# Which of the state-space products GpSimd makes: pairs 0, 1, 3 in place of 0, 2, 4

## The reference

```
state = state * exp(dt[d] * A[d, n]) + (dt[d] * u[d]) * B[n]      # one step in time, 512 of them
y[d]  = sum over n of state * C[n]
y     = (y + D * u) * silu(z)          # z is the layer norm of x
x     = x + transpose(y)
```

## Time and profile before

| | us |
|---|---|
| timed runs, median (lowest, highest) | 506.89 (505.04, 507.24) |
| the profiled execution's own time | 503.0 |
| its span | 501.2 |
| VectorE busy | 469.0 |
| GpSimd busy | 453.0 |
| TensorE busy | 431.6 |
| ScalarE busy | 346.5 |

### The profile page before, as it was taken

One profiled execution on the slowest core, in us unless ns is written; L12 is line 12 of the kernel. 1 busy time (PEld: TensorE's weight loads), 2 busy tenths in 40 slices (PEclk: granted clock), 3 DMA queues, 4 the chain that ended last, 5 costly groups with the idle time before them and its releaser, 6 DMA issues.

```text
span 501.2 us, 4086 instructions
## 1 busy us (share of the span) xinstructions
PE 431.6 (86%) x1028; PEld 179.7 (36%) x1036; DVE 469.0 (94%) x368; ACT 346.5 (69%) x620; POOL 453.0 (90%) x237
## 2 busy tenths in 40 slices
PE   8749869998798669999898699879988989988797
PEld 4214323433343233434333243424433433343343
DVE  5899999999998999999998999999999977999895
ACT  2797746966579868897679767788788693643332
POOL 4379999989898999999998999999999959999992
PEclk9979989999799989999899989989999997989899
DMA  5799745429971000200981000000593000000002
GB/s 185 250 368 335 185 84 116 88 41 233 329 276 56 0 1 0 63 1 27 332 339 43 1 21 1 21 1 0 166 397 157 1 21 21 32 11 21 1 0 84
DMA packets 17871, 53.96 MB, mean 108 GB/s; under 512 B 2724, under 2 KB 3236, under 8 KB 16824
## 3 DMA queue, kind: packets, MB, share of 16 engines
q1 hardware_dynamic: 16696, 45.31, 25.0%
q0 software_dynamic: 1152, 8.39, 8.3%
HBM read 49.24 MB, written 4.46 MB: 107 GB/s over the span
## 4 chain that ended last, share of the span: by engine, by line
POOL 36%; PE 21%; DVE 19%; issue 17%; ACT 4%; DMA 1%; SPq 0%; POOLq 0%; DVEq 0%; ACTq 0%
POOL h L1104 24%; PE y L509 10%; POOL h L1097 9%; DVE dA L953 9%; DVE h L959 3%; DVE h L953 3%; PE work L486 2%; POOL dtu L1090 2%; PE work L409 2%; ACT dA L774 2%; DVE acc L910 1%; PE work L502 1%; PE work L429 1%; DMA w_in<-w_inT 1%; PE work L436 1%
## 5 line engine op out<-in xcount | busy, mean ns | idle before, releaser
L1104 POOL TENSOR_TENSOR h<-b_rep,dtu 128x1024 f32<-128x1024 f32 x127 | 301.8, 2441 | 12.5 <-DMA b_rep<-bc_scratch 11.2
L509 PE MATMUL y<-h,ident 128*128 128x512 f32 x508 | 248.4, 627 | 37.2 <-DVE h L959 35.0
L774 ACT ACTIVATE dA<-dt,a_neg 128x512 f32<-128x512 f32 x256 | 165.7, 679 | 85.1 <-DVE h L959 74.9
L953 DVE TENSOR_TENSOR_SCAN dA<-dA,h 128x1024 f32<-128x1024 f32 x83 | 189.7, 2285 | 4.8 <-ACT dA L774 4.8
L509 PEld LDWEIGHTS y<-h,ident 128*128 128x128 f32 x508 | 96.3, 198 | 173.9 <-issue 108.6
L1097 POOL TENSOR_TENSOR h<-h,c_rep 128x1024 f32<-128x1024 f32 x45 | 107.1, 2382 | 11.8 <-DVE h L953 11.7
L953 DVE TENSOR_TENSOR_SCAN h<-dA,h 128x1024 f32<-128x1024 f32 x45 | 102.5, 2280 | 4.5 <-ACT dA L774 4.5
L959 DVE TENSOR_TENSOR h<-dA,c_rep 128x1024 f32<-128x1024 f32 x82 | 99.8, 1217 | 1.2
L409 PE MATMUL work<-ctx_sb,w_in 128*128 128x512 f32 x60 | 35.0, 716 | 15.1 <-DVE x L995 14.3
L502 PE MATMUL work<-fsum,xnT 128*128 128x512 f32 x64 | 29.2, 598 | 0.0
L910 DVE SCALAR_TENSOR_TENSOR acc<-work,chan,acc 128x511 f32<-128x511 f32 (+2 forms) x30 | 21.7, 731 | 5.3 <-ACT acc L641 5.0
(11 more groups left out here) (132 smaller groups left out, 415.1 us busy)
## 6 DMA issues: line engine op xcount, KB each, us to landing
b_rep<-bc_scratch SPq DMA_DIRECT2D x32, 512.0 KB, 9.3
c_rep<-bc_scratch SPq DMA_DIRECT2D x32, 512.0 KB, 9.0
fsum<-factors POOLq DMA_DIRECT2D x8, 1024.0 KB, 8.2
x<-x SPq DMA_DIRECT2D x4, 1024.0 KB, 8.5
out<-x SPq DMA_DIRECT2D x16, 256.0 KB, 2.0
ctx_sb<-ctxT SPq DMA_DIRECT2D x3, 512.0 KB, 4.1
ctx_sb<-ctxT SPq DMA_DIRECT2D x2, 256.0 KB, 3.8
w_in<-w_inT SPq DMA_DIRECT2D x1, 384.0 KB, 4.4
```

The costliest lines, as they stand in the source:

```text
L509: mm = pe.matmul(y[:], ident[:], h[:, (s * PAIRS + j) % H_RING, i, :], start=False, stop=(j == sum_order(s)[-1] and i == 1))
L774: act.activation(dA[:, j % 2, i, :], dt[:, k % 2, :], ACT.Exp, scale=a_neg[:, k, 2 * j + i:2 * j + i + 1]).then_inc(exp_done, 1)
L953: dve.tensor_tensor_scan(pair if on_pool(s * PAIRS + j) else decay, decay, pair, 0.0, ALU.mult, ALU.add).then_inc(scanned, 1)
L1104: pool.tensor_tensor(h[:, (s * PAIRS + j) % H_RING], b_rep[:, j], dtu[:, k % 2, :].unsqueeze(1).to_broadcast([P, 2, L]), ALU.mult).then_in ...
```

## The change

Four constants are replaced. In steps 0 to 3 GpSimd makes the products with C of pairs 0 and 3 in place of 0 and 4. In steps 4 to 14 it makes those of 0, 1 and 3 in place of 0, 2 and 4. In step 15 nothing changes. VectorE makes all others; which tile the scan writes, what ScalarE waits for and what SyncE waits for follow from `on_pool`. The orders of the sums on TensorE are changed with it.

```diff
-EARLY_POOL_C = (0, 4)
-EARLY_SUM_ORDER = (1, 0, 2, 3, 5, 4, 6, 7)
-POOL_C = (0, 2, 4)
+EARLY_POOL_C = (0, 3)
+EARLY_SUM_ORDER = (1, 0, 2, 4, 3, 5, 6, 7)
+POOL_C = (0, 1, 3)
 LAST_POOL_C = (0, 2, 4, 5)
-SUM_ORDER = (1, 0, 3, 2, 5, 4, 6, 7)
+SUM_ORDER = (0, 2, 1, 4, 3, 5, 6, 7)
 LAST_SUM_ORDER = (1, 0, 3, 2, 4, 6, 5, 7)
```

## The result

The changed kernel is slower. In the first measurement its median was 512.98 us (510.57 to 514.53) against 505.97 for the old one: ratio 1.0151, 95% interval 1.0104 to 1.0198. In a second one, on other runs, 1.0189 (1.0164 to 1.0213). So +7.6 to +9.5 us, where +4.4 was forecast. The median of 512.98 lies in the stated range, the sign was right and so was most of the mechanism; the size of the change was too small by a third or more.

What follows compares the result with a forecast made beforehand. VectorE, busy 94% of the span, was taken as the bound. Terms 1.0 + 3.9 - 0.7 + 1.7 - 1.5 = +4.4 us on the profiled 503.0 gave 507.4, carried over to 511.3 us timed; range 507.6 to 514.2.

Steps and rivals of the forecast that it cites:

- The pins in even steps: Steps 4, 6, 8, 10: ScalarE's block fixes pair 4's scan, whose product with C now lies behind it; +3.9 us.
- The joints: Steps 1 to 3, 5, 7, 9, 11: VectorE's product straight behind its own scan; +0.14 us each, +1.0 us in all.
- Steps 12 and 13: TensorE idles before pair 4's sum, then runs slow, delaying the last layer and step 13; +1.7 us.
- Steps 10 and 11: Pair 1 summed third instead of pair 3, so x_proj starts sooner and two gaps on VectorE go; -0.7 us.
- Steps 14 and 15: Sums of pairs 4 and 3 fill TensorE's gap, so step 15's gate of step 14's y starts sooner; -1.5 us.
- what costs nothing: GpSimd's reordered products, as many as before, and SyncE's shifted loads: most of GpSimd's 11.7 us waiting goes, at no cost.
- rival C: GpSimd or the loads become late, 1 to 2 us each time; slower still, 515; chance 0.07.
- Rival A: Decays in even steps move forward with VectorE, so waits at pairs 4 and 5 go; faster, 501.7 us; chance 0.07.
- E3: ScalarE's two decay exponentials of pair 3; starting over 1.1 us earlier in steps 4, 8 and 12 would favour Rival A.
- Rival B: Pins cost as forecast, but TensorE stays fast in step 12 and gives it back; no change, 508.0; chance 0.20.
- The sum's ends: Terms' extremes: 3.2 us at TensorE's full clock; 8.0 without gains of steps 10, 11, 15 and step 13 at 2.9.
- the 1.2 us I gave it: Whole kernel: TensorE's throttled clock makes the total some 1.2 us dearer than at full clock.

Runs made afterwards that it cites:

- odd_only: Old kernel with the new pairs and sum order in steps 5, 7, 9, 11 and 13 alone; 3.6 us slower than the old kernel.
- even_only: Old kernel with the new pairs and sum order in steps 4, 6, 8, 10, 12 and 14 alone; 1 us more than the upper end of the expected +4.5 to +5.5.
- k0_pool045: Old kernel, but in steps 4, 8 and 12 GpSimd multiplies pairs 0, 4, 5 instead of 0, 2, 4; ratio 1.0007 to the old kernel.
- after_gate4: Changed kernel with ScalarE's four gates behind the decays of pair 4 instead of pair 3; ratio 1.0043 to the old kernel.
- early_only: Old kernel with the change in steps 0 to 3 alone; the expected +0.4 us lies in the measured interval.
- before_gate4: Old kernel with ScalarE's four gates behind the decays of pair 4 instead of pair 3; ratio 1.0018 to the old kernel.
- after_warm: Changed kernel with products of a zero matrix added where TensorE idled in steps 9 and 12; ratio 1.0071 to the old kernel.
- after_bias4: Changed kernel with GpSimd's second bias addition of step 13 one pair later, at pair 4 instead of 3; ratio 1.0105 to the old kernel.
- combined: Changed kernel with later gates, later bias addition and zero-matrix products in steps 5, 7, 9, 12 and 13; ratio 0.9937 to the old kernel, 502.9 us.

## Why the prediction was right, and what was mis-sized

- *The pins in even steps* (+3.9 us in steps 4, 6, 8, 10): shown by the traces. Behind S0, S4 of step 8 starts at 15.95 to 15.96 us and S4 of step 12 at 15.34 to 15.35 in the old kernel, odd_only, even_only and both profiles of the changed one, whichever pairs these steps have (all five with these heads at full clock), and S5 came 0.91 us later each in steps 6 and 8. Putting a product more ahead of the pin (k0_pool045) shortened the steps by 1.2 us. Moving the gates (after_gate4) gave back only 0.2 of the 0.91, as C2 then held up E4. Step 4 measured +0.49 and +1.18 instead of +1.26: in the first profile TensorE had run step 3 at a higher clock than in the earlier trace rows, so the pin itself came 0.8 sooner. early_only and odd_only, with the old pairs in step 4, show the same 0.79.
- *The joints* (+0.14 each): +0.13 to +0.16 in steps 1, 2, 3, 5, 7 and 9.
- *Steps 12 and 13* (+1.7): +1.77 and +1.55. The slow sum of pair 4 was there (granted clock 0.50 after 3.95 us of idling), and filling the gap took it away. The layer behind it came 2.4 us later against S0 of step 12, the upper end of the 1.2 to 2.4 given, and the wait for the raw layer shrank by 1.7 as allowed for. That the sum came out to 0.1 us is partly luck: early_only, with the old code, is 1.44 us shorter in these two steps.
- *Steps 10 and 11*: the two gaps went (-0.34 and -0.76 between scans), but the net was +1.8, not +0.3. The term that was mis-sized is S4 of step 10: I took the head of the chain, the last layer on TensorE, from the old trace, where step 10 began at full clock. The slow head costs 1.70 us. The old pairs don't cover it either: it costs them +1.7 in step 6 of odd_only and before_gate4 and in step 8 of early_only, and +1.34 in step 10 of k0_pool045, where S4 stands at the same 16.64 us behind S0 as in the changed kernel. What differs is how often it comes: step 10 had it in all six profiles with the new pairs there and no filling, and in one of six with the old pairs. With the head at full clock (after_warm) steps 10 and 11 are at +0.13, near the forecast.
- *Steps 14 and 15* (-1.5): the gain at the gate came (1.54 to 0.20 us of waiting) and was given back in the tail. Here the step "what costs nothing" failed: GpSimd, with 11.7 us of waiting for scans in the whole, stands still nowhere behind its wait for ScalarE in step 13, in either kernel, and its start there is set by ScalarE's chain behind S1 of step 13. In the changed kernel it began 9.95 us later and ended 10.5 us later, so what VectorE regains at the gate doesn't count; giving GpSimd work in its wait (after_bias4) took 2.4 us off the last wait. It is rival C in another place. The waits before the gate and the half gates vary with the old pairs too (together 3.5 to 5.3 us in six profiles, 4.6 in the old kernel's), so the 1.5 us itself is no firm number.
- Rival A is refuted: E3 and E4 of step 8 didn't move against S0. Rival B too: the clock fell in step 12, as the larger gap suggested.
- The sum's ends were added up wrongly. 3.2 us on 506.9 gives 510.1, not 508.5, and with the gains gone and step 13 at 2.9 the terms make 7.8, not 8.0, so 514.7. The stated range of 507.6 to 514.2 doesn't hang on it.
- On the Trainium skill's rule (TensorE: Matmul & The Clock Gate, Part 1: The HAM clock gate): the page has the throttled 1.2 GHz as the default, which activity releases, and the runs agree. The lower of the two levels came behind idle time (0.50 granted behind 3.95 us), and added activity brought 2.4 GHz back (1.00). But not each idle stretch was followed by it: TensorE idles 1.98 us before the head of step 10 in the old kernel as in the changed one, and the granted clock behind it was 1.00 in the one and 0.57 in the other. The clock bore on more of the loss than the 1.2 us I gave it: the fillings alone were worth 4 to 6 us.

What stays open: why heads are slow in some executions and not in others, and why that of step 10 is slow so much more often with the new pairs (in steps 6 and 8 together it was 3 of 11 heads with the old pairs and 3 of 14 with the new ones, leaving out step 6 of k0_pool045, where GpSimd held up the sums, and the filled ones of combined). So it is open too how much of odd_only's 3.6 us, and of the 3 to 5 us between forecast and measurement, comes from such heads and how much from the tail.

## What to carry to other kernels

On a saturated engine, moving equal work between places costs nothing only if both lie on the same side of each point that another engine fixes; find those points first (a wait whose releaser is in a block that doesn't depend on the saturated engine) and count the work ahead and behind. Look also whether the block waits for one of the moved pieces, as E4 came to wait for C2 once the gates stood behind it: then the point moves. A total of idle time on another engine says nothing of a stretch: look whether it has any between its last fixed wait and the end. And where the matrix engine idles more after a change, price the next long product at the lower clock, wherever its result heads a chain.

## What was not expected of the hardware

With small products of a zero matrix, 32 in step 9 (0.83 and 1.28 us in all) and 56 in step 12 (3.30 us), the granted clock behind them was 1.00 instead of 0.57 and 0.50, and the whole kernel 4 to 6 us faster, though TensorE did nothing useful in them.

A slow head costs an even step 1.7 us whichever of the two sets of pairs it has, and one and the same code meets it in some executions and not in others.
